# A Mamba-2 mixer with a dense layer behind it: the group norm's sums of squares turned on VectorE and through DRAM instead of on TensorE, and the last unit's products with the step sizes ahead of its scores

## The reference

```python
g = y * jax.nn.silu(gate)
gg = g.reshape(b, s, G, INTER // G)
var = jnp.mean(gg * gg, axis=-1, keepdims=True)
gg = gg * jax.lax.rsqrt(var + EPS)
out = gg.reshape(b, s, INTER) * norm_w
return jnp.einsum('bsi,oi->bso', out, out_proj_w)
```

## Time and profile before

| | |
|---|---|
| median of 3 runs | 1562.43 us (lowest 1560.64) |
| the profiled execution, its own time | 1560.34 us |
| its span, first to last instruction | 1558.3 us |
| mean granted TensorE clock | 0.995 |
| busy share of PE, DVE, ACT, POOL | 98%, 85%, 74%, 47% |
| DMA rate over the span | 145 GB/s |

### The profile page before, as it was taken

The page is one execution under the profiler, slowest core; times in us unless marked ns, Lnnn a source line. Parts: engine busy times, 40 slices in busy tenths (PEclk is TensorE's granted clock), DMA queues, the critical chain, the costliest instruction groups (busy, mean ns, idle before and its releaser), DMA issues.

```text
span 1558.3 us, 25903 instructions
## 1 busy us (share of the span) xinstructions
PE 1529.5 (98%) x9080; PEld 1294.6 (83%) x9080; DVE 1329.5 (85%) x1854; ACT 1146.8 (74%) x2022; POOL 730.4 (47%) x535
## 2 busy tenths in 40 slices
PE   7899999999999999999999999999999999999988
PEld 5678888888888888888888888888888888888877
DVE  6688888998889887998889988898879988899877
ACT  6887767875877677777687767777678767777753
POOL 2154544463545354455455545445544644545550
PEclk9899999999999999999999999999999999999999
DMA  4564445444444444554444454445444435444411
GB/s 156 181 214 148 157 129 167 157 148 137 153 153 151 140 150 131 166 163 125 154 154 153 135 161 144 144 154 164 125 153 163 159 120 160 145 150 153 143 44 55
DMA packets 131554, 228.37 MB, mean 147 GB/s; under 512 B 24160, under 2 KB 76128, under 8 KB 130912
## 3 DMA queue, kind: packets, MB, share of 16 engines
q1 hardware_dynamic: 131424, 226.70, 45.2%
HBM read 187.84 MB, written 38.80 MB: 145 GB/s over the span
## 4 chain that ended last, share of the span: by engine, by line
issue 53%; POOL 36%; PE 8%; ACT 1%; DVE 0%; DMA 0%; SPq 0%; POOLq 0%; ACTq 0%; DVEq 0%
POOL square_sum L1540 8%; POOL xdecay L1553 8%; POOL y L1546 8%; POOL w_low L1532 8%; POOL out_low L1571 5%; PE d_bank L841 0%; PE g_bank L809 0%; PE g_bank L811 0%; PE g_bank L810 0%; PE head_bank L291 0%; DMA alog<-a_log 0%; PE head_bank L830 0%; PE x_bank L819 0%; PE head_bank L848 0%; PE g_bank L906 0%
## 5 line engine op out<-in xcount | busy, mean ns | idle before, releaser
L1553 POOL TENSOR_TENSOR xdecay<-xdt,tables 128x384 f32<-128x384 f32 x128 | 138.2, 1098 | 459.0 <-DVE xdt L1357 443.6
L1080 ACT ACTIVATE scores<-scores,tables 128x128 f32<-128x128 f32 x1024 | 312.0, 389 | 0.0
L1259 DVE SCALAR_TENSOR_TENSOR hs<-x_bank,cols,hs 128x1022 f32<-128x1022 f32 x189 | 241.7, 1279 | 56.7 <-ACT hs L1092 52.2
L1546 POOL TENSOR_TENSOR y<-y,gate 128x512 f32<-128x512 f32 x128 | 185.3, 1468 | 196.2 <-DVE y L1328 196.2
L1092 ACT ACTIVATE hs<-x_bank,cols 128x1024 f32<-128x1024 f32 x63 | 76.1, 1208 | 246.8 <-PE x_bank L823 215.9
L809 PE MATMUL g_bank<-x_high,w_high 128*128 128x512 f32 x624 | 250.9, 402 | 0.0
L811 PE MATMUL g_bank<-x_high,w_low 128*128 128x512 f32 x624 | 243.3, 390 | 0.0
L810 PE MATMUL g_bank<-x_low,w_high 128*128 128x512 f32 x624 | 243.0, 390 | 0.0
L1532 POOL TENSOR_TENSOR w_low<-raw,w_high 128x512 fp32r<-128x512 f32 x139 | 186.5, 1342 | 102.1 <-ACT w_high L1070 102.0
L1291 DVE TENSOR_TENSOR scores<-scores,bc 128x1024 f32<-128x1024 f32 x128 | 170.7, 1344 | 1.7 <-ACT scores L1085 1.7
L819 PE MATMUL x_bank<-x_high,w_high 128*128 128x512 f32 x496 | 152.8, 389 | 2.2 <-issue 2.2
(11 more groups left out here) (229 smaller groups left out, 3316.9 us busy)
## 6 DMA issues: line engine op xcount, KB each, us to landing
scores<-sums_dram SPq DMA_DIRECT2D x128, 512.0 KB, 4.6
raw<-w_in SPq DMA_DIRECT2D x144, 256.0 KB, 2.8
blocks_dram<-blocks SPq DMA_DIRECT2D x62, 512.0 KB, 4.2
blocks<-blocks_dram SPq DMA_DIRECT2D x248, 128.0 KB, 2.8
grown_rows<-grown_dram SPq DMA_DIRECT2D x256, 96.0 KB, 2.8
out_raw<-w_out SPq DMA_DIRECT2D x64, 256.0 KB, 3.4
mixed<-x SPq DMA_DIRECT2D x8, 256.0 KB, 4.8
table_dram<-table SPq DMA_DIRECT2D x2, 1024.0 KB, 6.2
```

The costliest lines, as they stand in the source:

```text
L1080: op = s.activation(at, at, ACT.Relu, bias=col[:, r, c:c + 1], scale=-1.0)
L1259: v.scalar_tensor_tensor(out=hs[:, q % 2, :, i:], in0=x_bank[:, :, 0:SEQ - i], scalar=cols[:, q, TAPS - 1 - i:TAPS - i], in1=hs[:, q % 2, ...
L1546: pool.tensor_tensor(y[:, b], y[:, b], gate[:, q % 2, b], ALU.mult).then_inc(y_ready, 1)
L1553: pool.tensor_tensor(xdecay[:, b], xdt[:, b, 0:LATER], col.unsqueeze(3).to_broadcast([P, LATER, PAIR, HEAD_DIM]), ALU.mult)\
```

## The change

The seven `turn_squares` of the loop go away, and with them PE's waits for `square_added`, for the next gate, and for `var_done`. In their place, in unit 1 of the next group, behind `to_heads`: DVE turns `square_sum` in 32x32 blocks into the tile `blocks` (`block_squares`), sums each block's 32 columns into `parts` (128x32), SP stores `parts` to DRAM and loads it back in four pieces as `quarters` (token rows, 4 partial sums for each of 8 tiles), and DVE sums these (`sum_quarters`) behind its `add_carry`. `group_std` and `group_rstd` move from unit 1 to unit 2, and so do the two `normed_out` of unit 1: unit 2 now has five. ACT's square of unit 0 into `square_sum` waits for `squares_blocked` (DVE's block turn) where it waited for `squares_turned` (PE). In the last unit `to_heads` stands at the head of DVE's list.

```diff
+            def store_parts(done):
+                sp.wait_ge(parts_ready, done)
+                sp.dma_start(squares_dram[done], parts[:].rearrange("p j n -> p (j n)")).then_inc(parts_stored, 16)
+
+            def load_quarters(done):
+                sp.wait_ge(parts_stored, 16 * done)
+                reached(sp, var_done, done - 1)
+                by_token = squares_dram[done].rearrange("(q t) (j n) -> j t q n", t=BLOCK, j=QUARTERS)
+                for i in range(QUARTERS):
+                    sp.dma_start(quarters[i * BLOCK:(i + 1) * BLOCK], by_token[i]).then_inc(quarters_in, 16)
...
+                    if j == 1 and g > 0:
+                        store_parts(g)
                     if ahead:
                         if ahead[2] < ALL - 1:
                             store_blocks(ahead[2])
+                            if j == 1 and g > 0:
+                                load_quarters(g)
                             load_heads(ahead[2])
...
-                        if j == 1:
-                            reached(pe, var_done, g)
...
-                    if j == 0 and g > 0:
-                        pe.wait_ge(square_added, (UNITS - 1) * g)
-                        pe.wait_ge(gate_ready, BATCH * (k + 2))
-                        turn_squares(square_sum)
...
                 if q == 0:
-                    reached(s, squares_turned, g)
+                    reached(s, squares_blocked, g)
                     s.activation(square_sum[:], y[:], ACT.Square).then_inc(squared, 1)
...
-                    if j == 1 and g > 0:
+                    if j == 2 and g > 0:
                         group_std(g)
...
+            def block_squares(done):
+
+                v.wait_ge(square_added, (UNITS - 1) * done)
+                v.wait_ge(xdt_ready, BATCH * (UNITS * done + 2))
+                v.transpose(blocks[:], square_sum[:].rearrange("p b (c j t) -> p j (b c) t", j=QUARTERS, t=BLOCK))\
+                 .then_inc(squares_blocked, 1)
+                v.wait_ge(squares_blocked, done)
+                reached(v, parts_stored, 16 * (done - 1))
+                v.tensor_reduce(parts[:], blocks[:], mybir.AxisListType.X, ALU.add).then_inc(parts_ready, 1)
+
+            def sum_quarters(done):
+                v.wait_ge(quarters_in, 16 * QUARTERS * done)
+                reached(v, std_ready, done - 1)
+                v.tensor_reduce(squares[:], quarters[:].rearrange("p q n -> p n q"), mybir.AxisListType.X, ALU.add)\
+                 .then_inc(var_done, 1)
...
-                    if k == 0:
+                    if k in (0, ALL - 1):
                         for b in range(BATCH):
                             to_heads(g, j, k, b)
-                    if j == 1 and g > 0:
-                        squares_of(g)
...
-                    if k > 0:
+                    if 0 < k < ALL - 1:
                         for b in range(BATCH):
                             to_heads(g, j, k, b)
                     if j == 1 and g > 0:
+                        block_squares(g)
+                    if j == 2 and g > 0:
                         group_rstd(g)
                     if g > 0:
-                        for at in {1: (0, 1), 2: (2, 3, 4), 3: (5, 6, 7)}.get(j, ()):
+                        for at in {2: (0, 1, 2, 3, 4), 3: (5, 6, 7)}.get(j, ()):
                             normed_out(g, at)
...
+                    if j == 1 and g > 0:
+                        sum_quarters(g)
                     if k > 1:
                         add_outs(g, j, (0, 1))
```

More of the change, by code:

```diff
@@ L101, in build @@
     blocks_dram = scratch("blocks_dram", [2, P, BATCH * SEQ])
+    squares_dram = scratch("squares_dram", [GROUPS, P, QUARTERS * BATCH * CHUNKS])
     x_tokens = x.rearrange("b (c p) d -> p (b c) d", p=P)
@@ L137, in build @@
         mixer(nc, first, banks, x_high, x_low, mixed, ident, causal, eps_col, buffers, loads, counts, w_in,
-              conv_bc, unit_cols, w_out, bias, dense_dram, blocks_dram, sums_dram, grown_dram, table_dram, chunk_dram,
+              conv_bc, unit_cols, w_out, bias, dense_dram, blocks_dram, squares_dram, sums_dram, grown_dram, table_dram, chunk_dram,
               out_tokens)
@@ L598, in mixer @@
 def mixer(nc, first, banks, x_high, x_low, mixed, ident, causal, eps_col, buffers, loads, counts, w_in, conv_bc,
-          unit_cols, w_out, bias, dense_dram, blocks_dram, sums_dram, grown_dram, table_dram, chunk_dram, out_tokens):
+          unit_cols, w_out, bias, dense_dram, blocks_dram, squares_dram, sums_dram, grown_dram, table_dram, chunk_dram,
+          out_tokens):
     x_bank, g_bank, d_bank, heads = banks
@@ L632, in mixer @@
         g_std, g_rstd, squares = sb("g_std", [P, TB]), sb("g_rstd", [P, TB]), sb("squares", [P, TB])
+        parts, quarters = sb("parts", [P, QUARTERS, TB]), sb("quarters", [P, QUARTERS, TB])
         last_squares, norm_bias = sb("last_squares", [P, TB]), sb("norm_bias", [P, TB])
@@ L666, in mixer @@
         blocks_ready, blocks_stored, heads_in = (sem(n) for n in ("blocks_ready", "blocks_stored", "heads_in"))
+        squares_blocked, parts_ready, parts_stored, quarters_in = (
+            sem(n) for n in ("squares_blocked", "parts_ready", "parts_stored", "quarters_in"))
         block = ctx.enter_context(nc.Block())
@@ L1385, in normed_out @@
                                        in1=mixed[:, at], op0=ALU.mult, op1=ALU.add).then_inc(mixed_ready, 1)
+            def block_squares(done):
[11 more added lines that the diff above has]
+                 .then_inc(var_done, 1)
             def squares_of(done):
-                v.wait_ge(squares_turned, done)
+                v.wait_ge(squares_turned, 1)
                 reached(v, std_ready, done - 1)
@@ L1393, in last_squares_of @@
             def last_squares_of():
-                v.wait_ge(squares_turned, GROUPS + 1)
+                v.wait_ge(squares_turned, 2)
                 v.tensor_reduce(last_squares[:], g_bank[:].rearrange("p b (c l) -> p (b c) l", c=CHUNKS),
```

## The result

The changed kernel takes 1613.55 us (median of 5 runs, 1613.39 to 1614.56); the kernel before takes 1561.71 us on the same chip. The ratio is 1.0339, with a 95% interval of 1.0328 to 1.035: 51.8 us between the medians, 3.4% slower by the ratio. One of the five executions of the kernel before took 3133 us, twice the others, and the ratio leaves it out. The forecast was 1596, with 1573 to 1609 as its range. The direction and the places were right, and the time is above the range.

The account below looks back on a forecast made before the run. PE, busy 98% of the span, sets the time. Seven groups lose 4.35 + 1.3 us each (39.6), the last unit wins 5.3: +34.3 on 1560.34, plus 2.1 for the median; forecast 1596, range 1573 to 1609.

Parts of the forecast that it names:

- What leaves PE: In the group loop: each turn of transposes costs PE 0.88 us, seven cost 6.2; the wait for `var_done` costs nothing.
- unit 1: DVE's block turn delays ACT's square and `tap0`; PE waits 0.4 us, leaving unit 1 only 0.5 us ahead of before.
- The way through DRAM: Quarters land at 286.4, so DVE begins unit 2 1.6 us late and PE waits about 1 us for `x_bank`.
- Unit 2: Two extra `normed_out` add 3.05 us, the reciprocal 0.2; PE is 4.35 us later at `carry` per group (1.4 to 6.4).
- The clock: Behind PE's 3.9 us idle before unit 2's `carry`, a lower granted clock costs nothing to 1.7 us, 1.3 in the mean.
- rival 1: The same waits, but the clock stays up behind PE's idle time: +25 us, 1588; chance 0.20.
- The last unit: `to_heads` ahead of the scores removes PE's wait for `xdecay` and the low clock: 5.3 us won (4 to 5.6).
- the fourth: DRAM slower still, and both `normed_out` and POOL stretch each other: more than 6.5 us per group, 1610 and above; chance 0.10.

Follow-up runs that it names:

- The move alone: The kernel before, transposes and sum kept; only root, reciprocal and the two `normed_out` of unit 1 move to unit 2, which has five: 1603.87 us, ratio 1.0277.
- the addition in halves: The changed kernel with POOL's addition to `square_sum` as two instructions of 512 columns instead of one of 1024: 1603.64 us, ratio 1.028.

## Why the prediction was too low

**What leaves PE** and **unit 1** were right. The forecast had PE 0.5 us ahead behind unit 1, and it is 22.04 - 21.65 = 0.39. ACT's square, `tap0` and a wait of 0.4 came as described (0.35). The steps on DVE lasted 1.25 and 1.22, as taken from the nearest rows.

**The way through DRAM** was right in its sum by luck, since two errors cancel. "Even with the 4.2 of a large store they have landed by about 282": the store went out only at 279.28 and took 5.0 us, so SP waited until 285.1. "I take 3.2" for the loads: they took 1.7. The runs with another order on the queue changed both with the sizes as they were: 5.0 to 2.5 for the store, 1.7 to 2.3 for the loads. Whether it is the place on the queue or the traffic at that moment, no run separates. DVE waited 1.76 us in the mean, where the forecast had 286.4 - 284.4 = 2.0. The 2.0 us of fixed cost that the forecast quotes from the Trainium skill (DMA: Bandwidth & Descriptors, the anatomy of one DMA) stand there for DMAs that GpSimd issues, and SP issues these; the runs show 1.7 for the loads and 5.0 for the store.

**The step that failed is in "Unit 2": "I take five of 1.25, which adds 3.05".** From DVE's add out of `d_bank` to the last state it is 309.06 + 0.86 - 289.48 = 20.44 us; before it was 14.96. That is 5.48 more, not 3.25 with the reciprocal, and lies outside "3.9 for further stretch". The three durations of the earlier trace rows (739, 1325, 1331) were read as "POOL idle" and "beside POOL", as if a busy POOL cost a fixed 0.6 us. They were one turn beside an `xdecay` of 1.24 us. The price of a turn is the length of the POOL instruction, and the extra two reached an instruction of 2.8 us. The rows for it stood in the trace of the kernel before, in POOL's timeline of unit 2:

```profile
291.86 2.47 POOL L1553 TENSOR_TENSOR xdecay<-xdt,tables 128x384 f32<-128x384 f32 x2 [5.62 <-DVE xdt L1357]
295.03 1.66 POOL L1532 TENSOR_TENSOR w_low<-raw,w_high 128x512 fp32r<-128x512 f32 x1 [0.70 <-ACT w_high L1070]
296.65 2.37 POOL L1540 TENSOR_TENSOR square_sum<-square_sum,gate 128x1024 f32<-128x1024 f32 x1
```

The third `normed_out` fell into the gap of 0.70 us; a fourth and a fifth meet `w_low` and `square_sum`. The move alone (6.2 per group), the same five ahead of `y_low` (3.40 us) and the addition in halves (7.42) show this term, its place and its mechanism, each by itself.

The Trainium skill has the rule (SBUF — State Buffer, "Who interferes with whom"): a VectorE instruction with two inputs in SBUF and a GpSimd instruction that reads SBUF contend for a pair of ports under an exclusive lock, held for the whole instruction, while the other engine is blocked. The runs agree on the blocking, 2.85 us against 1.76 for the halved addition. They show a shorter hold on POOL's side: its rows grow by 0.43 us beside a `normed_out` that lasts 0.74 alone. By that rule the forecast could have counted turns: `xdecay`, `xdecay`, the gap, `w_low` and `square_sum`, which is the 7.47 of the move alone. The last 1.04 came when DVE's lateness closed the gap.

**The clock**: "I take 1.3 as the mean of the seven". With waits of 5.7 us in place of 3.9 it came to 0.50 each time; by the intervals behind `carry`, it cost 14.5 / 7 = 2.1 us, above the upper bound of 1.7. Even with a wait of 3.8 us (the move alone) it never held, so rival 1 is refuted.

**The last unit**: 5.3 expected, 4.8 alone and 5.0 inside the change. The 0.3 named for the late score is 0.57, since the score takes turns with `xdecay` too.

Per group the forecast had 4.35 + 1.3 = 5.65; the intervals give (45.9 + 14.5 - 2.7) / 7 = 8.2. `normed_out` accounts for 2.2 of the difference and the clock for 0.8; the quarters, waiting 1.76 and costing PE less at `x_bank` than thought, take back about 0.4. Of the rivals the fourth was the nearest, and its second half ("both `normed_out` and POOL stretch each other") is what happened. Its first half, slower DRAM, was not needed. It had 0.10: the forecast priced contention from durations and not from which instructions meet.

The Trainium skill's rule that speaks against turning squares on VectorE (VectorE: DVE Perf Modes, rules for kernel authors) did not decide. With the same 2.7 us of DVE work in unit 0 the transposes do come out with a gain; the place of the turn and of the norms made the loss.

## What to carry to other kernels

When instructions are moved on VectorE in front of something TensorE waits for, lay GpSimd's timeline beside the new place and count turns: here each `normed_out`, with its two SBUF inputs, waited out the GpSimd instruction that it met, from 1.24 to 2.81 us. Look first for places behind the last instruction that TensorE waits for; there the same norms and block turns cost TensorE 0.4 us per group. And price a wait of TensorE by its length and the slow stretch behind it together: 3.8 us of waiting cost 6 here.

## What the runs showed of the hardware

- A `scalar_tensor_tensor` of 128x512 in float32 with two SBUF tensors takes 0.74 us while POOL is idle, 1.33 beside an instruction of 1.24, 1.76 beside one of 1.72 and 2.85 beside one of 2.81. POOL pays too: 1.29 becomes 1.72, 2.37 becomes 2.81. DVE's taps, which read one input from PSUM, last 3.90 for three, with POOL at work beside them or not.
- Smaller instructions on POOL shorten DVE's wait though POOL takes longer: 2.81 in one piece, 3.42 in two, DVE 1.1 us earlier.
- The same store of 16 KB landed in 5.0 us behind two loads of 512 KB, in 2.5 ahead of them, and in 1.7 and 1.8 in the two runs with it in unit 0, 3 us behind such loads. The loads of 4 KB took 1.7 to 2.3.
- Behind waits of 3.7 to 5.7 us `carry` took 2.93 us instead of 1.50, the granted clock being 0.50 for 3.0 to 6.2 us from its start. In three groups (waits of 4.0 and 4.6 us, two runs) the clock fell only 0.4 to 0.6 us after `carry` had begun, and it took 2.45 to 2.63. Behind waits of 2.2 and 2.4 us for `xdecay` the clock fell in three groups, behind the other four, of 1.6 to 2.1, it did not; it fell behind one wait of 1.9 at `x_bank`. Behind waits of 0.2 to 1.8 us `carry` took 1.60.
